# Attention's first query weights: two more pieces split in the first stage, and output weights split two steps sooner

## The reference, cut to what matters

```
xn = layernorm(x)                                  # 2048 x 512
q = (xn @ Wq)      # 512 -> 32 heads of 128, in 4 groups of 8 that share keys and values
k, v = (concat(ctx, xn) @ Wk), (... @ Wv)          # 4 heads of 128, 128 keys in each batch
p = softmax(q k^T / sqrt(128))
x = x + tanh(g_xattn) * ((p v) @ Wo)
x = x + tanh(g_ffn) * moe(layernorm(x))            # router, top 2 of 16 experts, shared expert
```

## Time and profile before

| | |
|---|---|
| median of 3 runs | 1467.69 us (1464.2 to 1468.52) |
| span of the profiled execution | 1485.9 us |
| TensorE (PE) matmul busy | 1416.6 us, 95% of the span |
| TensorE weight loads (PEld) | 1253.0 us, 84% |
| VectorE (DVE) | 1041.1 us, 70% |
| ScalarE (ACT) | 785.9 us, 53% |
| GpSimd (POOL) | 191.1 us, 13% |
| DMA | 230.98 MB, mean 155 GB/s |

### The profile page before, as it was taken

The page is one execution under the profiler, slowest core; times in us unless marked ns, Lnnn a source line. Parts: engine busy times, 40 slices in busy tenths (PEclk is TensorE's granted clock), DMA queues, the critical chain, the costliest instruction groups (busy, mean ns, idle before and its releaser), DMA issues.

```text
span 1485.9 us, 24374 instructions
## 1 busy us (share of the span) xinstructions
PE 1416.6 (95%) x8624; PEld 1253.0 (84%) x8624; DVE 1041.1 (70%) x1682; ACT 785.9 (53%) x2029; POOL 191.1 (13%) x200
## 2 busy tenths in 40 slices
PE   7999988999999999999999999999998899989885
PEld 6888887999999899999899999899997588888774
DVE  4422238777788777787877787887787587656657
ACT  4212226555566555566655566655555445767660
POOL 0000000000000000000000000000026124777740
PEclk9999999999999999999999999999999999999998
DMA  8576555344454433463443365444324206876419
GB/s 264 156 231 170 142 198 157 123 135 125 149 179 146 139 121 121 161 180 127 142 150 118 123 179 167 133 136 138 119 90 144 99 1 211 258 252 212 150 29 339
DMA packets 189622, 230.98 MB, mean 155 GB/s; under 512 B 22675, under 2 KB 123063, under 8 KB 185418
## 3 DMA queue, kind: packets, MB, share of 16 engines
q1 hardware_dynamic: 179530, 212.77, 45.3%
q0 software_dynamic: 9984, 16.82, 3.5%
HBM read 161.85 MB, written 83.36 MB: 165 GB/s over the span
## 4 chain that ended last, share of the span: by engine, by line
PE 67%; DVE 6%; ACT 5%; issue 3%; DMA 2%; another core or an unknown queue 2%; SPq 0%; ACTq 0%; POOL 0%; DVEq 0%; POOLq 0%
PE ps_q L84 8%; PE ps_y L84 8%; PE ps_y L86 7%; PE ps_y L85 7%; PE ps_q L85 7%; PE ps_q L86 7%; PE ps_s L1082 5%; PE bank L84 3%; PE bank L86 3%; PE bank L85 2%; PE ps_s L1084 2%; PE ps_o L84 2%; PE ps_o L86 2%; PE ps_o L85 2%
## 5 line engine op out<-in xcount | busy, mean ns | idle before, releaser
L84 PE MATMUL ps_q<-xt,wq_hi 128*128 128x256 f32 x1024 | 296.3, 289 | 2.3 <-PEq L119 1.7
L85 PE MATMUL ps_q<-xt,wq_lo 128*128 128x256 f32 x1024 | 289.4, 283 | 0.0
L86 PE MATMUL ps_q<-xt,wq_hi 128*128 128x256 f32 x1024 | 289.4, 283 | 0.0
L903 ACT ACTIVATE s_sb<-s_sb,nmax 128x128 f32<-128x128 f32 x512 | 200.5, 394 | 148.5 <-DVE nmax L991 148.5
L84 PE MATMUL ps_y<-wo_hi,o_hi 128*128 128x512 f32 x512 | 204.6, 400 | 7.2 <-DVE wo_lo L935 3.6
L86 PE MATMUL ps_y<-wo_lo,o_hi 128*128 128x512 f32 x512 | 203.5, 398 | 0.0
L85 PE MATMUL ps_y<-wo_hi,o_lo 128*128 128x512 f32 x512 | 202.6, 396 | 0.0
L84 PEld LDWEIGHTS ps_q<-xt,wq_hi 128*128 128x128 f32 x1024 | 195.2, 191 | 2.9 <-issue 2.1
L85 PEld LDWEIGHTS ps_q<-xt,wq_lo 128*128 128x128 f32 x1024 | 195.8, 191 | 0.0
L86 PEld LDWEIGHTS ps_q<-xt,wq_hi 128*128 128x128 f32 x1024 | 195.6, 191 | 0.0
L883 ACT ACTIVATE o_hi<-ps_o 128x512 fp32r<-128x512 f32 x128 | 76.1, 595 | 183.2 <-PE ps_o L86 183.0
(11 more groups left out here) (261 smaller groups left out, 3160.2 us busy)
## 6 DMA issues: line engine op xcount, KB each, us to landing
xt<-x_scratch SPq DMA_DIRECT2D x32, 1024.0 KB, 5.6
p_table<-p_blocks SPq DMA_DIRECT2D x128, 256.0 KB, 2.0
p_lo<-p_table SPq DMA_DIRECT2D x512, 64.0 KB, 2.1
w_raw<-in_L_ffn_ew SPq DMA_DIRECT2D x93, 256.0 KB
v_full<-v_out SPq DMA_DIRECT2D x64, 128.0 KB, 2.6
k_full<-k_out SPq DMA_DIRECT2D x16, 512.0 KB, 2.8
w_raw<-in_L_xattn_Wq SPq DMA_DIRECT2D x16, 512.0 KB, 5.9
kt_raw<-k_full SPq DMA_DIRECT2D x32, 256.0 KB, 2.8
```

The lines of the kernel that those rows point to most:

```text
L84: pe.matmul(out, w_hi, x_hi, start=first, stop=False)
L85: pe.matmul(out, w_lo, x_hi, start=False, stop=False)
L86: return pe.matmul(out, w_hi, x_lo, start=False, stop=last)
L903: last = act.activation(s_sb[:, i], s_sb[:, i], ACT.Exp, bias=nmax[:, i:i + 1], accum_out=sums[:, i:i + 1])
```

## The change

Stage one now splits two more pieces: piece 1 next to piece 0 behind octet 2, and piece 2, which SP loads into the first raw buffer in unit 0 of octet 3 and which is split behind octet 3's last copy (ScalarE) and behind the second key copy (VectorE). SP also loads piece 3 there, in unit 1. At the start of stage two the three splits are now those of pieces 3, 4 and 5, and SP loads kt_raw, xt and vt_raw ahead of pieces 4 and 5. In the steps, pieces 6 and 7 are split in steps 0 and 1, where pieces 4 and 5 were; steps 2 and 3 have no split. The lines by which SP loads pieces 6 and 7 in steps 0 and 1 are not changed.

```diff
--- before.py
+++ after.py
@@ -108,7 +108,8 @@
         wk_raw = Buffers(nc, before).sb("wk_raw", [P, 2, 1024])
     xt0 = h.sb("xt0", [P, 2, C, 256], F32R)
     wq0 = [h.sb(f"wq_{part}0", [P, C, 256], F32R) for part in ("hi", "lo")]
-    common.update(w_raw=w_raw, xt0=xt0, wq0=wq0, raw_in=[s.sem(f"raw_in{i}") for i in range(2)],
+    wq1, wq2 = [[h.sb(f"wq_{part}{i}", [P, C, 256], F32R) for part in ("hi", "lo")] for i in (1, 2)]
+    common.update(w_raw=w_raw, xt0=xt0, wq0=wq0, wq1=wq1, wq2=wq2, raw_in=[s.sem(f"raw_in{i}") for i in range(2)],
                   xt_in=[s.sem(f"xt_in{i}") for i in range(2)], w_hi_made=s.sem("w_hi_made"),
                   w_lo_made=s.sem("w_lo_made"), kt_in=s.sem("kt_in"))
     wq_v = a["L0_xattn_Wq"].rearrange("(c p) (g n) -> g p c n", p=P, g=NKV)
@@ -206,6 +207,11 @@
                         sp.dma_start(ctx_raw[:, 0], ctx_v[o + 1][:, 0]).then_inc(ctx_in[0], 16)
                         sp.dma_start(ctx_raw[:, 1:4], ctx_v[o + 1][:, 1:4]).then_inc(ctx_in[1], 16)
 
+                    if o == OCTETS - 1 and u < 2:
+                        sp.wait_ge(common["w_lo_made"], u + 1)
+                        sp.dma_start(first_piece(w_raw[u]), wq_v[0, :, :, 512 + 256 * u:768 + 256 * u]
+                                     ).then_inc(common["raw_in"][u], 16)
+
                     sp.wait_ge(v_copied, UNITS * o + u + 1)
                     for bb in range(2):
                         batch = (i % 2) * 2 + bb
@@ -306,8 +312,11 @@
                     act.activation(gain_attn[:], gates[:, 0:1], ACT.Tanh)
                     act.activation(gain_ffn[:], gates[:, 1:2], ACT.Tanh)
                 if o == 2:
-                    act.wait_ge(common["raw_in"][0], 16)
-                    act.activation(wq0[0][:], first_piece(w_raw[0]), ACT.Copy).then_inc(common["w_hi_made"], 1)
+                    for i, wq in enumerate((wq0, wq1)):
+                        act.wait_ge(common["raw_in"][i], 16)
+                        act.activation(wq[0][:], first_piece(w_raw[i]), ACT.Copy).then_inc(common["w_hi_made"], 1)
+            act.wait_ge(common["raw_in"][0], 32)
+            act.activation(wq2[0][:], first_piece(w_raw[0]), ACT.Copy).then_inc(common["w_hi_made"], 1)
 
         @block.vector
         def _(dve):
@@ -380,6 +389,10 @@
                     rstd_of(4, 8, 2)
                 for job in range(UNITS):
                     k_copy(o, job)
+                    if o == OCTETS - 1 and job == 1:
+                        dve.wait_ge(common["w_hi_made"], 3)
+                        dve.tensor_tensor(wq2[1][:], first_piece(w_raw[0]), f32(wq2[0][:]),
+                                          ALU.subtract).then_inc(common["w_lo_made"], 1)
                     if o == 0 and 2 <= job < 6:
                         if job % 2 == 0:
                             dve.wait_ge(x_in[1 + job // 2], 16)
@@ -391,9 +404,10 @@
                     if o + 1 < OCTETS and job == 4:
                         tok_low(o + 1, 0)
                 if o == 2:
-                    dve.wait_ge(common["w_hi_made"], 1)
-                    dve.tensor_tensor(wq0[1][:], first_piece(w_raw[0]), f32(wq0[0][:]),
-                                      ALU.subtract).then_inc(common["w_lo_made"], 1)
+                    for i, wq in enumerate((wq0, wq1)):
+                        dve.wait_ge(common["w_hi_made"], i + 1)
+                        dve.tensor_tensor(wq[1][:], first_piece(w_raw[i]), f32(wq[0][:]),
+                                          ALU.subtract).then_inc(common["w_lo_made"], 1)
 
         @block.tensor
         def _(pe):
@@ -660,7 +674,7 @@
     keep = Buffers(nc, common["kept"])
     with ExitStack() as stack:
         b = Buffers(nc, stack)
-        wq_hi, wq_lo = [[common["wq0"][k]] + [b.sb(f"wq_{part}{i}", [P, C, 256], F32R) for i in range(1, 4)]
+        wq_hi, wq_lo = [[common[f"wq{i}"][k] for i in range(3)] + [b.sb(f"wq_{part}3", [P, C, 256], F32R)]
                         for k, part in enumerate(("hi", "lo"))]
         wo_hi = b.sb("wo_hi", [P, HG, D], F32R)
         wo_lo = b.sb("wo_lo", [P, HG, D], F32R)
@@ -738,7 +752,7 @@
         def splits_at(t, o, j):
 
             if at_end(t):
-                return [4 + j] if t == 0 and j < 4 else []
+                return [6 + j] if t == 0 and j < 2 else []
             if isinstance(o, int) and o == 3 and 1 <= j <= 4:
                 return [j - 1]
             if o == 0 and j in (2, 3, 4):
@@ -783,18 +797,16 @@
                     sp.dma_start(f32(p_lo[m % 2][BLOCK * j:BLOCK * j + BLOCK]),
                                  p_table[m % 2, :, :, j].rearrange("i k c -> k i c")).then_inc(p_in[m % 2], 16)
 
-            for i in range(2, 6):
-                load_piece(0, i)
-                if i == 3:
-                    load_kt(0, 0)
-                    load_xt(1, 1)
-                    load_vt(0, 0)
-                if i == 5:
-
-                    sp.wait_ge(k_lo_made, 1)
-                    load_kt(0, 1)
-                    sp.wait_ge(v_lo_made, 1)
-                    load_vt(0, 1)
+            load_kt(0, 0)
+            load_xt(1, 1)
+            load_vt(0, 0)
+            load_piece(0, 4)
+            load_piece(0, 5)
+
+            sp.wait_ge(k_lo_made, 1)
+            load_kt(0, 1)
+            sp.wait_ge(v_lo_made, 1)
+            load_vt(0, 1)
 
             def octet(t, o, g):
                 fetches = not at_end(t)
@@ -917,7 +929,7 @@
 
             for i in range(4):
                 if i < 3:
-                    split_piece(0, i + 1)
+                    split_piece(0, i + 3)
                 if i == 3:
                     keys_hi(0, 0)
                 query_hi(0, 0, i)
```

## The result

The changed kernel takes 1481.77 us (median; 1477.75 to 1485.55) against 1465.95 us (1461.45 to 1468.52) for the kernel before, measured side by side: a ratio of 1.0115 with a 95% interval of 1.0091 to 1.0139, that is 16.9 us (13 to 20) lost; the two medians lie 15.8 us apart. 1481.3 and +13.65 had been forecast.

A forecast was written before the change was run, and what follows sets the result against it. TensorE, full from near 243 us, was taken as the bound, so ramp delays move the end: 0.2 + 1.0 + 6.0 + 6.6 - 0.15 = 13.65 us, added to the median 1467.69, gives 1481.3 us; range 1475 to 1487.

The forecast's parts named there:

- main step: Steps 0 and 1: splits of pieces 6 and 7 wait for loads issued behind that step's store, +6.0 and +6.6 us.
- rival of one stall in place of two: Steps 0 and 1: piece 7's wait is mostly covered, so only +7.5 us, 1475; 8 in 100.
- 0.2 us of stage one: Stage one: piece 1's low half delays VectorE's token subtraction and the TensorE job reading it, 0.2 us lost (0 to 0.3).
- start of stage two: First queries: pair 3 waits for piece 4 to land, because its split precedes pair 1's copy; +1.0 us (0 to 3.2).
- landing of piece 4: Start of stage two: piece 4's load was expected to land at 210.0, bounds 209.0 and 212.2.
- rival at step 4: Ramp: TensorE's half clock after longer idle times reaches past step 4's start, up to 4 us more, 1485.5; 12 in 100.
- term that was won back: Steps 2 and 3 without splits: gain of 0.15 us (0 to 1.13), with TensorE at half clock as the limit.
- gain that the edit looks for: Ramp: pieces 6 and 7 are there when ScalarE reaches them, about -2.6 us, 1465.1; 3 in 100.
- piece 5 is late for nobody: Start of stage two: only copies behind piece 5's split use it, and they wait for pair 3 anyway; no cost.
- ramp isn't made up for later: Stage two behind step 4: the rival claimed slack there absorbs the late start, no change, 1467.7; 3 in 100.

The follow-up runs named there:

- piece 6 alone: Changed kernel with only the load of piece 6 moved ahead of the steps, piece 7 still loaded behind step 1's store: 1473.81 us, ratio 1.0064.
- both edits: Changed kernel with loads of pieces 6 and 7 ahead of the steps and query copies ahead of the splits of pieces 4 and 5: 1468.30 us, ratio 1.0025.
- piece 4 first: Changed kernel with SP's load of piece 4 put ahead of kt, xt and vt at the start of stage two: 1478.90 us, ratio 1.0105.

## Why the prediction was right, and which terms were off

The main step is shown: pieces 6 and 7, split two places sooner with their loads left behind the store of the same step, cost a stall each. +6.0 and +6.6 had been worked out from the row of that store, the time to landing and the spacing of the splits; it was +5.91 and +6.43 in the trace, and taking the two loads away from behind the stores takes away 5.91 and 6.43. The rival of one stall in place of two falls by the run with piece 6 alone.

The 0.2 us of stage one were 0.25: the value job that reads the token tile started at 154.03 + 3.21 before and at 155.36 + 3.46 after. SP's loads and the split of piece 2 there were hidden, as said.

The step that was mis-sized is the start of stage two: +1.0 with bounds of 0 to 3.2, and +5.09 in the trace, outside them. Two things were wrong in it. The landing of piece 4 had been put at 210.0 in the clock of before, from the 2.0 us by which vt and piece 4 followed xt; it was 205.47 + 7.7 = 213.2, less the offset of 1.60 that is 211.6, inside the bounds but 1.6 later. And I let pair 3 take as long as before however late it starts: the starts of its matmuls spanned 2.76 us before. TensorE had been idle for 3.31 us by then, ran pair 3 at half clock, and took 221.30 - 216.25 = 5.05 for the same; the clock had been priced only as a rival at step 4. The wait comes to about 2.7 us and the clock to about 2.4. This is one execution: with the same start of stage two the fold of step 0 was 3.1 us late with pieces 6 and 7 loaded early, and 2.2 us late, with no fall of the clock, with piece 6 alone. So the term is 2.2 to 5.1 us in three profiles, of which the wait is 1.6 to 2.7 and the clock 0.1 to 2.4.

The term that was won back was mis-sized too, the other way: 0.15 forecast (the working, 1.72 less 1.4, gives 0.3), 11.13 - 10.01 = 1.12 measured. I expected the half-clock stretch of the earlier trace rows to repeat behind the longer idle time. TensorE met less of it: from 252.65 to about 256.1, 3.4 us, against 5.8 before (233.61 to about 239.4). Both stretches lasted some 6.8 us in all, and in both profiles the clock fell while TensorE stood still, but before the change only some 1.0 us ahead of its first matmul, and after it some 3.4 us ahead. The clock of before:

```profile
231.00:233.00 2.00, 0.00 (x0) 0.00 (x0) 1.97 (x4) 0.57 (x2) 0.00 (x0) 0.90 0.70 226
...
239.00:241.00 2.00, 1.97 (x15) 1.76 (x14) 1.97 (x4) 0.53 (x3) 0.00 (x0) 0.89 0.56 169
```

So after the change a larger part of the half-clock stretch lay in the idle time, the queries of step 3 were not late, and VectorE's missing split in step 3 counted in full. The runs without splits in steps 2 and 3 bear this out: where TensorE ran at half clock for 3.4 to 3.7 us behind the first product with the values, it took 10.0 us from the fold of step 2 to the scores of step 4; with piece 6 alone, some 5 us of it, 10.59; with both edits, 6.4 us, 11.19, and nothing was won. Together: 0.27 + 5.09 + 5.91 + 6.43 - 1.12 = 16.6 and not 13.65.

That the median came out within 0.5 us of the forecast is partly luck: the start of stage two was put 4.1 us too low and what is won back 1.0 too low, which partly cancel, and the median of before was 1465.95 in the comparison and not 1467.69, which hid 1.7 of the 3 us by which the sum was short; and the two medians are 15.8 us apart where the trace has 16.6. The Trainium skill, page "DMA: Bandwidth & Descriptors", section "Anatomy of one DMA — SWDGE (gpsimd) path", whose fit was set beside the rows in the prediction, gives an estimate of 3.2 us for such a load and would have been off by more: 4.3 and 4.8 us were measured on SP's queue, and 7.7 behind 1.5 MB on the same queue.

Of the rivals, the gain that the edit looks for shows in the trace once the loads are moved and the splits of pieces 4 and 5 as well, and is 1.9 us in size, but in the times it can't be told from no change. That piece 5 is late for nobody held in the changed kernel, where the wait for piece 4 covered it; with both edits it held back the copy of pair 3, and with piece 4 first that of pair 2. The ramp isn't made up for later: from step 4's scores to the end of stage two both profiles take 912.5 us. The clock did cost time, as a rival had named, but 2.4 us at pair 3 and not up to 4 at step 4. What decides when the clock falls and how long it stays down is open; no run here was made for it.

## What to carry to other kernels

When the consumer of a load is moved forward in a loop, move the issue with it, and look at what the issue stands behind on its queue: here it stood behind a store that waits for the same step's result, so the lead was not short but negative. A transfer waited for by an in-order engine costs what is queued behind the waiting instruction, so a split should stand behind the copies that others need, not ahead of them. And a wait that leaves TensorE idle can cost twice: for itself, and for the work behind it at half clock (2.7 and 2.4 us here); 2.77 us of it in another run cost no clock, so the second price is not always paid.

## What was not expected of the hardware

TensorE's clock fell to 0.50 behind shorter idle times than the 4.14 us of before: 3.31 us in the changed kernel, 2.80 with piece 4 first, 2.40 with both edits, 2.24 with pieces 6 and 7 loaded early. The length of the idle time alone doesn't decide it: behind 2.77 us with piece 6 alone the clock stayed at 1.00. How long TensorE then ran at half clock differed too (3.4 to 6.4 us behind the first product with the values), because the clock had fallen earlier or later in the idle time or, in some runs, after it. With both edits, the 2.40 us of waiting cost another 1.5 us between the folds of steps 0 and 1.
